# Linear attention: the inverted normalizer copied to each head's channels by eight DMAs

## The chip, the cores and the metric

The kernel runs on one core of a Trainium2 chip. The metric is the time of one execution in microseconds, as the device measures it. The program is one launch that computes two transformer layers one phase after the other: softmax attention, a router with 16 experts, linear attention, and a coupling network. The change touches only the third of these.

## What is computed

Of the reference, this is the part that the change is about (here for one sequence; the kernel does it for 8 sequences of 512 tokens with 256 channels, 16 heads of 16 channels each):

```python
q_prime = elu(q) + 1.0
k_prime = elu(k) + 1.0
kv_cumsum = cumsum(einsum('bhld,bhle->bhlde', k_prime, v), axis=2)
context = einsum('bhld,bhlde->bhle', q_prime, kv_cumsum)
k_cumsum = cumsum(k_prime, axis=2)
norm = einsum('bhld,bhld->bhl', q_prime, k_cumsum)
output = context / (norm[..., None] + EPS)
return output.reshape(b, l, e) @ out_w + out_b
```

`norm` has one value for each head and token; the context has 16 channels for each head. So the inverse of `norm` must stand 16 times, once for each channel of its head, before the context can be multiplied by it.

## The kernel before

`linear_phase` (L1357) works through 8 sequences, b = 0 to 7. Every engine runs the same list of steps, built by `placed_order` from the table `LINEAR_PLACE` (L1281): a step of sequence b stands at place 36 b plus its number in the table, so steps of two or three sequences are woven into each other. Each engine does its own part of a step and waits on semaphores for the parts of others. Within an engine everything runs in the order of the list.

The steps are: `ln` SyncE loads x (512 KB) and a gate row; `st` DVE takes the moments of a later sequence; `xn` ACT normalizes; `hT` PE transposes and ACT copies out (two halves); `qk` PE makes q and k, ACT and DVE map them; `v` PE and DVE; `mask` ACT; `nt` the normalizer; `A` PE makes the scores of 128 tokens and DVE masks them (L1612, four instructions) in four tiles; `kt`, `KV` the running state; `PV` PE makes the context of 128 tokens in psum and DVE multiplies it by the inverted normalizer into `oN` (L1648); `pr` PE projects (L1833), DVE adds the residual (L1656), and SyncE stores (L1442).

The normalizer goes this way. PE sums over each head's channels (L1760): the result has heads and token tiles in its partitions, row 32 i + 8 k + h for token tile i, channel half k and head h of that half, and 128 tokens in the free dimension. DVE adds 1e-6 and inverts it into `rinv` (L1599, L1603, semaphore `inverted`). GpSimd multiplies it by a mask that leaves one block of rows for each token tile (`rdiag`, L1522). In step `nb`, two halves k, PE multiplies a constant 0/1 matrix by `rdiag` (L1767), which puts each head's row on its 16 channels for all 512 tokens, in psum bank 6 (`ps_x`), and ACT copies that to `rb` (L1722, `l_norm_rows` in the trace). The first `PV` of the sequence on DVE waits for that copy.

Psum bank 6 is shared by `hT`, `qk`, `nb` and `kt`: each of them on PE waits until ACT has copied out the one before. Psum bank 7 (`ps_y`) is shared by `v`, `nt` and `pr` in the same way with DVE.

In the order around the change the steps of a sequence b run: `nt`, `kt`, `KV`, `v`, `A` 0, `nb` 0, `pr` 2 of b-1, `hT` 0 of b+1, `A` 1, `pr` 3 of b-1, `nb` 1, `PV` 0, `hT` 1 of b+1, `A` 2, `KV` 1, `pr` 0, `PV` 1, and then `qk` and `v` of b+1. On SyncE's queue stand, from this stretch, the stores of `pr` and the load of b+2, which waits for `pr` 3 of b-1. After `pr` 3 of sequence 0 the queue also issues nine loads of the next phase's weights (L1447), and after `pr` 3 of sequence 2 one load of 1 MB (L1451).

Of the kernel before, what the change touches and what calls it, by code (L numbers as in the profile page):

```python
# [24 lines left out]
P = 128  # L25
# [13 lines left out]
C_SPREAD = C_HEADS + KC * 32  # L39
C_TILES = C_SPREAD + KC * P  # L40
C_END = C_TILES + NT

# [16 lines left out]
def shape_constants():  # L59
# [14 lines left out]
    for k in range(KC):  # L74
        c[i, C_HEADS + k * 32 + 8 * k + i // HD] = 1
        for h in range(8):
            c[i % 32 == 8 * k + h, C_SPREAD + k * P + h * HD:C_SPREAD + k * P + (h + 1) * HD] = 1
    c[i, C_TILES + i // 32] = 1
# [37 lines left out]
def placed_order(table, count, steps, sequences):  # L116

    def place(s):
        at = table[s[0]]
        for n in s[1:]:  # L120
            at = at[n]
        return at

    assert len(steps) == count
    order = [(count * b + place(s), (s[0], b) + s[1:]) for b in range(sequences) for s in steps]
    return [s for _, s in sorted(order)]
# [878 lines left out]
def expert_phase(nc, m):  # L1005
# [284 lines left out]
    "nb": [48, 53],  # L1290
# [8 lines left out]
def linear_steps():  # L1299

    steps = [("ln",), ("st",), ("xn",), ("nt",)]
    steps += [(kind, n) for kind in ("hT", "mask", "nb") for n in range(2)]
    steps += [(kind, n) for kind in ("qk", "v", "A", "PV", "pr") for n in range(4)]
    return steps + [(kind, n) for kind in ("kt", "KV") for n in range(NT - 1)]
# [52 lines left out]
def linear_phase(nc, m):  # L1357
# [4 lines left out]
    x_use, _ = index_of(order, ("hT", "qk", "nb", "kt"))  # L1362
    y_use, _ = index_of(order, ("v", "nt", "pr"))
    QK_PLACE = {2: 0, 0: 1, 3: 2, 1: 3}
    with ExitStack() as ctx:
# [24 lines left out]
        rdiag = sb("l_norm_diag", [P, NT, P])  # L1390
# [15 lines left out]
        spread = m.const[:, C_SPREAD:C_SPREAD + KC * P].rearrange("p (k c) -> p k c", k=KC)  # L1406
        tiles = m.const[:, C_TILES:C_TILES + NT]
# [11 lines left out]
        placed = sem("lin_norm_placed")  # L1419
# [8 lines left out]
        with nc.Block() as block:  # L1428
            @block.sync
            def _(sp):  # L1430
                for s in order:
                    if s[0] == "ln":
# [5 lines left out]
                        sp.dma_start(rowb[:, b % 3, :], m.mod_rows[b:b + 1, ROW_GATE_L1 * C:(ROW_GATE_L1 + 1) * C].to_broadcast([P, C])).then_inc(in_loaded[b % 3], 16)  # L1438
                    if s[0] == "pr":
# [14 lines left out]
            def _(pool):  # L1454
# [18 lines left out]
                def step(s):  # L1473
# [40 lines left out]
                    if s[0] == "nt":  # L1514
                        b = s[1]
                        pool.wait_ge(inverted, b + 1)
                        settle(pool, m.passed)
                        if b:

                            pool.wait_ge(x_fill, x_use[("nb", b - 1, 1)] + 1)  # L1520
                            settle(pool, m.passed)
                        pool.tensor_tensor(rdiag[:], rinv[:].unsqueeze(1).to_broadcast([P, NT, P]),  # L1522
                                           tiles.unsqueeze(2).to_broadcast([P, NT, P]), ALU.mult).then_inc(placed, 1)
# [14 lines left out]
            def _(dve):  # L1538
# [17 lines left out]
                def step(s):  # L1556
# [39 lines left out]
                    if s[0] == "nt":  # L1596
# [4 lines left out]
                        if b:  # L1601
                            dve.wait_ge(placed, b)
# [35 lines left out]
                    if s[0] == "PV":  # L1638
# [3 lines left out]
                        if i == 0:  # L1642

                            dve.wait_ge(x_drain, x_use[("nb", b, 1)] + 1)
# [17 lines left out]
            def _(act):  # L1662
                def step(s):
# [52 lines left out]
                    if s[0] == "nb":  # L1716
                        _, b, k = s
                        act.wait_ge(x_fill, x_use[s] + 1)
                        if b >= 2:

                            act.wait_ge(o_norm, NT * (b - 1))
                        act.activation(rb[:, b % 2, k, :], ps_x, ACT.Copy).then_inc(x_drain, 1)  # L1722
# [5 lines left out]
            def _(pe):  # L1728
                def step(s):
# [33 lines left out]
                    if s[0] == "nb":  # L1763

                        _, b, k = s
                        pe.wait_ge(placed, b + 1)
                        pe.matmul(ps_x, spread[:, k, :], rdiag[:].rearrange("p i t -> p (i t)"), start=True,  # L1767
                                  stop=True).then_inc(x_fill, 1)
# [656 lines left out]
```

## Time and profile before

| | us |
|---|---|
| median of 3 runs (1177.37 to 1180.38) | 1179.05 |
| span of the profiled execution, first to last instruction | 1175.3 |
| what lies around the span (median less span) | 3.75 |
| linear attention, from about 720 to 983 in the span | 263 |
| PE busy over the span | 1067.3 (91%) |
| DVE, ACT, GpSimd busy | 734.6, 596.7, 467.8 |

All times in the trace are from the start of the span. The time of the profiled execution as a whole is not listed apart from its span, so the 3.75 us around it are taken from the median of the runs. An engine's busy time in a stretch says how close it is to being the limit there; the idle time ahead of an instruction in the timeline, and what ended it, says for whom it waited.

### The profile page before, as it was taken

Reading aid. Unit: us, or ns where it says so; the run is one execution under the profiler, and the core shown is the slowest. Engines: PE = TensorE matmul, PEld = TensorE weight load, DVE = VectorE, ACT = ScalarE, POOL = GpSimd, SP = SyncE. Lnnn points to the kernel's source line nnn. Section 1 sums busy time; section 2 is a strip of 40 time slices with the busy share of each in tenths; the row PEclk is TensorE's granted clock in tenths of the full one; section 3 lists DMA queues with packets and bytes.
Section 4 is the critical chain, followed back from the end, with each engine's and each line's share of the span. In section 5 each row is a group of like instructions: output and inputs, shape, how many; then the busy total and the mean of one; then the engine's idle time right before and its main releaser. Section 6 shows DMA issues by size and latency. Waiting matters only on the chain. (4 is left out here: it accounts for less than half of the span.)

```text
span 1175.3 us, 19800 instructions
## 1 busy us (share of the span) xinstructions
PE 1067.3 (91%) x6630; PEld 603.4 (51%) x6630; DVE 734.6 (63%) x1549; ACT 596.7 (51%) x1133; POOL 467.8 (40%) x692
## 2 busy tenths in 40 slices
PE   5699999999999998479999974899999998999997
PEld 3244455454454443336565642566666665455654
DVE  2867878787787783624332322767787874566756
ACT  3167667676767666113332322443444442876752
POOL 2444635444453511068888874323333420000000
PEclk9599999999999999579999996999999998999999
DMA  4531414233250411436766672021210002001001
GB/s 150 99 58 18 87 37 89 65 70 82 52 105 21 73 40 47 155 103 138 162 162 135 138 154 71 6 65 42 76 39 26 35 15 95 1 10 63 28 28 54
DMA packets 73540, 85.05 MB, mean 72 GB/s; under 512 B 12560, under 2 KB 67800, under 8 KB 73312
## 3 DMA queue, kind: packets, MB, share of 16 engines
q1 hardware_dynamic: 61088, 66.99, 21.9%
q0 software_dynamic: 12288, 16.79, 8.4%
q8 instruction: 54, 0.88, 0.3%
q14 instruction: 46, 0.38, 0.1%
q10 hardware_dynamic: 64, 0.02, 0.0%
HBM read 45.31 MB, written 25.21 MB: 60 GB/s over the span
## 5 line engine op out<-in xcount | busy, mean ns | idle before, releaser
L566 DVE TENSOR_REDUCE nmax<-psum 128x1 f32<-128x512 f32 (+3 forms) x352 | 215.6, 637 | 44.6 <-PE psum L790 39.8
L683 ACT ACTIVATE pT<-psum 128x512 f32<-128x512 f32 x320 | 181.2, 596 | 65.5 <-PE psum L811 35.5
L788 PE MATMUL psum<-k6T,q6T 96*128 96x512 bf16 (+3 forms) x512 | 128.7, 312 | 15.2 <-DVE nmax L566 11.3
L808 PE MATMUL psum<-q6T,k6T 99*128 99x512 bf16 x320 | 119.3, 382 | 1.1 <-ACT pT L683 0.9
L1093 POOL DMA_INDIRECT residual<-expert_y,idx_e x64 | 101.3, 1583 | 25.2 <-issue 17.1
L1612 DVE TENSOR_TENSOR l_scores<-psum,const_sb 128x512 f32<-128x512 f32 x128 | 79.5, 684 | 19.1 <-PE psum L1787 19.0
L788 PEld LDWEIGHTS psum<-k6T,q6T 96*128 96x128 bf16 x512 | 46.0, 100 | 88.4 <-DVE nmax L566 55.2
L790 PE MATMUL psum<-negs_bf,ident_bf 128*128 128x128 bf16 (+2 forms) x352 | 89.0, 253 | 0.0
L823 PE MATMUL psum<-pT,v 128*32 128x512 f32 x640 | 85.0, 604 | 0.0
L1080 POOL DMA_INDIRECT expert_tokens<-router_input,idx_e x64 | 63.2, 987 | 50.0 <-POOLq L913 30.8
L1745 PE MATMUL psum<-l_hT,l_w 128*128 128x512 f32 x128 | 66.4, 643 | 1.6 <-ACT l_hT L1680 0.9
L2252 PE MATMUL psum<-c_x0T,c_w 128*128 128x512 f32 x128 | 62.2, 619 | 0.0
L1147 PE MATMUL psum<-expert_h,expert_w 128*128 128x512 f32 x128 | 61.2, 623 | 0.5 <-ACT expert_h L1193 0.5
L1689 ACT ACTIVATE l_plus_one<-psum,l_bone 128x512 f32<-128x512 f32 x32 | 22.0, 688 | 74.3 <-PE psum L1745 71.8
L1147 PE MATMUL psum<-expert_tokensT,expert_w 128*128 128x512 f32 x128 | 59.1, 604 | 0.3 <-DVE expert_tokensT L1236 0.3
L808 PEld LDWEIGHTS psum<-q6T,k6T 99*128 99x128 bf16 x320 | 31.1, 99 | 46.1 <-ACT pT L683 28.2
L1260 DVE TENSOR_TENSOR expert_y<-expert_weighted,gb_rows 128x256 f32<-128x256 f32 x64 | 27.3, 427 | 40.4 <-ACT expert_weighted L1205 36.3
L1205 ACT ACTIVATE expert_weighted<-psum,par_e 128x256 f32<-128x256 f32 x64 | 30.9, 564 | 41.3 <-PE psum L1175 37.5
L811 PE MATMUL psum<-negt_bf,ident_bf 128*128 128x512 bf16 x128 | 48.6, 380 | 0.0
L1252 DVE TENSOR_SCALAR expert_h<-psum,par_e 128x512 f32<-128x512 f32 x16 | 12.0, 751 | 58.1 <-PE psum L1147 58.1
L2039 POOL TENSOR_SCALAR c_vtmp<-c_mv 128x8 f32<-128x8 f32 x3 | 0.7, 241 | 116.8 <-DVE c_mv L2075 116.8
L2266 PE MATMUL psum<-c_a,c_w 128*128 128x512 f32 x96 | 45.2, 602 | 1.6 <-ACT c_a L2217 1.6
(298 smaller groups left out, 2245.4 us busy)
## 6 DMA issues: line engine op xcount, KB each, us to landing
q6T<-q_parts SPq DMA_DIRECT2D x96, 128.0 KB, 4.3
expert_w<-in_ew SPq DMA_DIRECT2D x16, 768.0 KB
x_in<-in_x SPq DMA_DIRECT2D x8, 512.0 KB, 4.2
residual<-x SPq DMA_DIRECT2D x32, 128.0 KB, 1.9
router_input<-h SPq DMA_DIRECT2D x32, 128.0 KB, 1.8
l_x<-residual SPq DMA_DIRECT2D x8, 512.0 KB, 6.6
x_dram<-l_x SPq DMA_DIRECT2D x32, 128.0 KB, 1.7
out<-c_out SPq DMA_DIRECT2D x16, 256.0 KB, 2.1
```

The lines of the kernel that those rows point to most:

```text
L566: dve.tensor_reduce(nmax[:, i, u * nh:(u + 1) * nh], ps_s[:, n % SR, 0:nh * (i + 1) * P].rearrange("p (h k) -> p h k", h=nh), AX_X, ALU.ma ...
L683: act.activation(pT[:, n % PR].rearrange("p h t -> p (h t)"), ps_t[:, n % TR, :], ACT.Exp, scale=HD ** -0.5).then_inc(probs, 1)
L788: pe.matmul(out[:, a, :], q6T[0:6 * HD, b % 2, u * nh + a, i * P:(i + 1) * P], k6T[0:6 * HD, b % 2, 0:w], start=a == 0, stop=False, skip_g ...
L790: pe.matmul(out[:, :, i * P:w], m.ident_bf[:], m.negs_bf[:].unsqueeze(1).to_broadcast([P, nh, P]), start=False, stop=True, skip_group_chec ...
L808: last = pe.matmul(out, k6T[:, b % 2, j * P:(j + 1) * P], q6T[:, b % 2, hg * 4:hg * 4 + 4, i * P:(i + 1) * P], start=True, stop=j < i)
L823: last = pe.matmul(ps_o[32 * hg:32 * hg + 32, :], v32[:, b % 2, j, :], pT[:, (n + hg) % PR].rearrange("p h t -> p (h t)"), start=j == 0, s ...
L1080: pool.indirect_dma_start(out=tok[:, e % TOK, i, :], out_offset=None, in_=tokens, in_offset=bass.IndirectOffsetOnAxis(ap=m.idx_e[:, e, i:i ...
L1093: pool.indirect_dma_start(out=rows, out_offset=bass.IndirectOffsetOnAxis(ap=m.idx_e[:, e, i:i + 1], axis=0), in_=y[:, e % YS, i, :], in_of ...
L1147: ins = pe.matmul(ps[:, o, :], wts[:, e % 2, n, k, o * P:(o + 1) * P], src[:, k, :], start=k == 0, stop=k == KC - 1)
L1612: dve.tensor_tensor(kept[:, t % 2, r, :].rearrange("p (h t) -> p h t", h=4), ps_a[:, r, :].rearrange("p (h t) -> p h t", h=4), keep.unsque ...
L1745: last = pe.matmul(ps_x, w[:, k, n * P:(n + 1) * P], hT[:, k, :], start=k == 0, stop=k == KC - 1)
L2252: last = pe.matmul(ps_1[:, n % 2, :], w1[:, w, k, h * P:(h + 1) * P], o[:, q % 3, a, k, :], start=k == 0, stop=k == KC - 1)
```

## The change

The step `nb` is gone from the table, and with it GpSimd's block diagonals, the PE multiplications, ACT's copies out of psum and the two constants `spread` and `tiles`. Psum bank 6 has two users less. In their place SyncE, at place `nt`, waits for `inverted` and issues eight DMAs, one for each token tile and channel half: each reads 8 partitions of `rinv` (one row of 128 floats for each of 8 heads) 16 times over and writes 128 partitions of `rb`, 512 bytes each. All count on one semaphore, `spread`. The first `PV` of the sequence on DVE waits until all eight have landed, and so does DVE before it overwrites `rinv` one sequence later.

```diff
-    "nb": [48, 53],
@@ constants
-C_SPREAD = C_HEADS + KC * 32
-C_TILES = C_SPREAD + KC * P
-C_END = C_TILES + NT
+C_END = C_HEADS + KC * 32
@@ sync
+                    if s[0] == "nt":
+                        b = s[1]
+                        sp.wait_ge(inverted, b + 1)
+                        if b >= 2:
+
+                            sp.wait_ge(o_norm, NT * (b - 1))
+                        for i in range(NT):
+                            for k in range(KC):
+                                lo = 32 * i + 8 * k
+                                sp.dma_start(rb[:, b % 2, k, i * P:(i + 1) * P],
+                                             rinv[lo:lo + 8, :].unsqueeze(1).to_broadcast([8, HD, P])).then_inc(spread, 16)
@@ gpsimd
-                        pool.tensor_tensor(rdiag[:], rinv[:].unsqueeze(1).to_broadcast([P, NT, P]),
-                                           tiles.unsqueeze(2).to_broadcast([P, NT, P]), ALU.mult).then_inc(placed, 1)
@@ vector, step nt
                         if b:
-                            dve.wait_ge(placed, b)
+                            dve.wait_ge(spread, 16 * NT * KC * b)
                         dve.reciprocal(rinv[:], npe[:]).then_inc(inverted, 1)
@@ vector, step PV
                         if i == 0:
 
-                            dve.wait_ge(x_drain, x_use[("nb", b, 1)] + 1)
+                            dve.wait_ge(spread, 16 * NT * KC * (b + 1))
@@ scalar
-                        act.activation(rb[:, b % 2, k, :], ps_x, ACT.Copy).then_inc(x_drain, 1)
@@ tensor
-                        pe.matmul(ps_x, spread[:, k, :], rdiag[:].rearrange("p i t -> p (i t)"), start=True,
-                                  stop=True).then_inc(x_fill, 1)
```

On PE, from `A` 0 of a sequence in the middle to `pr` 0, this is the order before (L1787 is `A`, L1767 `nb`, L1833 `pr`, L1740 `hT`, L1821 `PV`, L1800 `KV`):

```order
1609 L1787 MATMUL psum<-l_q_masked,l_k 128x256 x8
1610 L1767 MATMUL psum<-l_norm_diag,const_sb 128x512
1611 L1833 MATMUL psum<-l_gwo,l_oN 128x256 x2
1612 L1740 MATMUL psum<-const_sb,l_xn 128x128 x4
1613 L1787 MATMUL psum<-l_q_masked,l_k 128x256 x8
1614 L1833 MATMUL psum<-l_gwo,l_oN 128x256 x2
1615 L1767 MATMUL psum<-l_norm_diag,const_sb 128x512
1616 L1821 MATMUL psum<-l_scores,l_v 32x128 x16
1617 L1740 MATMUL psum<-const_sb,l_xn 128x128 x4
1618 L1787 MATMUL psum<-l_q_masked,l_k 128x256 x8
1619 L1800 MATMUL psum<-l_v,l_k_tokens 128x128 x2
1620 L1833 MATMUL psum<-l_gwo,l_oN 128x256 x2
```

and this is the same stretch of PE in the change, whose lines stand some 8 to 21 lower in the file:

```order
1605 L1766 MATMUL psum<-l_q_masked,l_k 128x256 x8
1606 L1812 MATMUL psum<-l_gwo,l_oN 128x256 x2
1607 L1725 MATMUL psum<-const_sb,l_xn 128x128 x4
1608 L1766 MATMUL psum<-l_q_masked,l_k 128x256 x8
1609 L1812 MATMUL psum<-l_gwo,l_oN 128x256 x2
1610 L1800 MATMUL psum<-l_scores,l_v 32x128 x16
1611 L1725 MATMUL psum<-const_sb,l_xn 128x128 x4
1612 L1766 MATMUL psum<-l_q_masked,l_k 128x256 x8
1613 L1779 MATMUL psum<-l_v,l_k_tokens 128x128 x2
1614 L1812 MATMUL psum<-l_gwo,l_oN 128x256 x2
```

The two multiplications into bank 6 are gone; nothing else on PE has changed its place.

On SyncE's queue, for the sequences 2 and 3, the change has (L1444 are the stores of `pr`, L1428 and L1429 the load of a later sequence, L1439 the new copies):

```order
228 L1428 DMA l_x<-residual 128x4x256 [waits lin_vector_bank_drained]
229 L1429 DMA l_rows<-mod_rows 128x256
230 L1444 DMA x3_dram<-l_x3 128x256 [waits lin_vector_bank_drained] x2
231 L1439 DMA l_norm_rows<-l_norm_inv 128x1x128 [waits lin_out_normalized,lin_norm_inverted]
232 L1439 DMA l_norm_rows<-l_norm_inv 128x1x128 x7
233 L1444 DMA x3_dram<-l_x3 128x256 [waits lin_vector_bank_drained] x2
234 L1428 DMA l_x<-residual 128x4x256 [waits lin_vector_bank_drained]
```

where before there were four stores between the loads:

```order
225 L1437 DMA l_x<-residual 128x4x256 [waits lin_vector_bank_drained]
226 L1438 DMA l_rows<-mod_rows 128x256
227 L1442 DMA x_dram<-l_x 128x256 [waits lin_vector_bank_drained] x4
228 L1437 DMA l_x<-residual 128x4x256 [waits lin_vector_bank_drained]
```

The eight copies stand between the second and the third store.

## Rows read from the trace of the kernel before

**Rows 1.** The linear phase as one window: busy us (and instructions) of each engine.

```profile
core 0: us, PE busy (x) PEld busy (x) DVE busy (x) ACT busy (x) POOL busy (x), PEclk, DMA share, GB/s
739.00:983.00 244.00, 237.66 (x2344) 158.04 (x2344) 181.94 (x387) 103.41 (x174) 79.04 (x100) 0.99 0.12 39
```

**Rows 2.** The inversion: durations min/median/max in ns, first and last start.

```profile
L1603 DVE RECIPROCAL l_norm_inv<-l_norm x8: 953/954/954, 740.2 to 960.2; 128x128 f32<-128x128 f32 x8
```

**Rows 3.** Timeline of PE, sequence 3: start, us, line, operation, [idle before].

```profile
838.19 1.10 PE L1767 MATMUL psum<-l_norm_diag,const_sb 128*128 128x512 f32 x2
839.13 1.03 PE L1833 MATMUL psum<-l_gwo,l_oN 128*128 128x256 f32 x4
...
840.56 1.33 PE L1787 MATMUL psum<-l_q_masked,l_k 32*128 32x256 f32 x16
...
842.79 1.02 PE L1767 MATMUL psum<-l_norm_diag,const_sb 128*128 128x512 f32 x2
843.74 1.08 PE L1821 MATMUL psum<-l_scores,l_v 128*32 128x128 f32 x32
...
846.42 0.71 PE L1800 MATMUL psum<-l_v,l_k_tokens 128*128 128x128 f32 x4
846.97 1.03 PE L1833 MATMUL psum<-l_gwo,l_oN 128*128 128x256 f32 x4
...
849.38 1.13 PE L1745 MATMUL psum<-l_hT,l_w 128*128 128x512 f32 x2
```

**Rows 4.** Timeline of DVE, sequence 3.

```profile
835.78 0.95 DVE L1603 RECIPROCAL l_norm_inv<-l_norm 128x128 f32<-128x128 f32 x1
...
838.23 2.48 DVE L1612 TENSOR_TENSOR l_scores<-psum,const_sb 128x512 f32<-128x512 f32 x4 [0.70 <-PE psum L1787]
...
841.80 2.49 DVE L1612 TENSOR_TENSOR l_scores<-psum,const_sb 128x512 f32<-128x512 f32 x4 [0.75 <-PE psum L1787]
...
844.89 0.42 DVE L1648 TENSOR_TENSOR l_oN<-psum,l_norm_rows 128x256 f32<-128x256 f32 x1 [0.28 <-PE psum L1821]
846.57 2.49 DVE L1612 TENSOR_TENSOR l_scores<-psum,const_sb 128x512 f32<-128x512 f32 x4 [1.26 <-PE psum L1787]
...
849.63 0.42 DVE L1648 TENSOR_TENSOR l_oN<-psum,l_norm_rows 128x256 f32<-128x256 f32 x1
```

**Rows 5.** SyncE's queue in softmax attention: six copies, SBUF to SBUF.

```profile
25.36 3.92 SPq L323 DMA_DIRECT2D q6T<-q_parts  x6
```

**Rows 6.** Landing of single 8 KB copies (L346) and of 128 KB stores (L1442).

```profile
DMA to landing us min/median/max: 1.7/1.7/2.7
...
DMA to landing us min/median/max: 1.7/1.7/4.6
```

**Rows 7.** Windows (last: DMA share, GB/s): within those six copies; loads from DRAM.

```profile
30.00:31.00 1.00, 0.00 (x0) 0.00 (x0) 0.99 (x2) 0.00 (x0) 0.77 (x4) 0.58 1.12 120
...
849.00:850.00 1.00, 1.00 (x20) 0.56 (x11) 1.00 (x4) 0.00 (x0) 0.00 (x0) 1.00 1.04 344
```

**Rows 8.** Inversions of the sequences 1 and 2, and the wait between them.

```profile
770.01 0.95 DVE L1603 RECIPROCAL l_norm_inv<-l_norm 128x128 f32<-128x128 f32 x1
...
789.65 0.17 DVE L1563 COPY l_cols<-modT 128x4 f32<-128x4 f32 x1 [5.37 <-DMA l_rows<-mod_rows]
...
805.06 0.95 DVE L1603 RECIPROCAL l_norm_inv<-l_norm 128x128 f32<-128x128 f32 x1
```

**Rows 9.** Idle stretches of PE, and PE's windows (busy, clock) after two of them.

```profile
793.89 1.27 PE L1751 MATMUL psum<-l_w,l_hT 128*128 128x256 f32 x4 [2.54 <-DVE l_v L1594]
...
1013.59 0.63 PE L2234 MATMUL psum<-const_sb,c_xn 128*128 128x128 f32 x4 [1.74 <-ACT c_xn L2148]
...
1014.00:1017.00 3.00, 2.84 (x15) 1.00 0.02 5
795.80:799.20 3.40, 3.40 (x24) 0.65 0.00 0
```

**Rows 10.** Step `qk` on PE after `PV` 1, sequence 0.

```profile
752.89 1.98 PE L1745 MATMUL psum<-l_hT,l_w 128*128 128x512 f32 x4
```

More of the change, by code:

```diff
@@ L75, in shape_constants @@
         c[i, C_HEADS + k * 32 + 8 * k + i // HD] = 1
-        for h in range(8):
-            c[i % 32 == 8 * k + h, C_SPREAD + k * P + h * HD:C_SPREAD + k * P + (h + 1) * HD] = 1
-    c[i, C_TILES + i // 32] = 1
     return c
@@ L122, in place @@
         return at
-    assert len(steps) == count
+    assert len(steps) <= count
     order = [(count * b + place(s), (s[0], b) + s[1:]) for b in range(sequences) for s in steps]
@@ L1301, in linear_steps @@
     steps = [("ln",), ("st",), ("xn",), ("nt",)]
-    steps += [(kind, n) for kind in ("hT", "mask", "nb") for n in range(2)]
+    steps += [(kind, n) for kind in ("hT", "mask") for n in range(2)]
     steps += [(kind, n) for kind in ("qk", "v", "A", "PV", "pr") for n in range(4)]
@@ L1361, in linear_phase @@
     order = [s for s in order if s not in LINEAR_LEAD]
-    x_use, _ = index_of(order, ("hT", "qk", "nb", "kt"))
+    x_use, _ = index_of(order, ("hT", "qk", "kt"))
     y_use, _ = index_of(order, ("v", "nt", "pr"))
@@ L1389, in linear_phase @@
         rinv = sb("l_norm_inv", [P, P])
-        rdiag = sb("l_norm_diag", [P, NT, P])
         rb = sb("l_norm_rows", [P, 2, KC, T])
@@ L1405, in linear_phase @@
         heads = m.const[:, C_HEADS:C_HEADS + KC * 32].rearrange("p (k h) -> p k h", k=KC)
-        spread = m.const[:, C_SPREAD:C_SPREAD + KC * P].rearrange("p (k c) -> p k c", k=KC)
-        tiles = m.const[:, C_TILES:C_TILES + NT]
         gated = sem("lin_residual_gated")
@@ L1418, in linear_phase @@
         inverted = sem("lin_norm_inverted")
-        placed = sem("lin_norm_placed")
+        spread = sem("lin_norm_spread")
         a_fill = sem("lin_scores_filled")
@@ L1513, in step @@
                         pool.tensor_tensor(qk[:, k, :], qs[:, b % 2, k, :], kc[:, k, :], ALU.mult).then_inc(multiplied, 1)
[L1514 to L1521, printed above, removed]
-                        pool.tensor_tensor(rdiag[:], rinv[:].unsqueeze(1).to_broadcast([P, NT, P]),
-                                           tiles.unsqueeze(2).to_broadcast([P, NT, P]), ALU.mult).then_inc(placed, 1)
                     if s == ("nt", 6):
@@ L1715, in step @@
                         act.activation(ktok[:, i, :], ps_x[:, 0:C], ACT.Copy).then_inc(x_drain, 1)
[L1716 to L1721, printed above, removed]
-                        act.activation(rb[:, b % 2, k, :], ps_x, ACT.Copy).then_inc(x_drain, 1)
                 for s in order:
@@ L1762, in step @@
                         last.then_inc(y_fill, 1)
-                    if s[0] == "nb":
-                        _, b, k = s
-                        pe.wait_ge(placed, b + 1)
-                        pe.matmul(ps_x, spread[:, k, :], rdiag[:].rearrange("p i t -> p (i t)"), start=True,
-                                  stop=True).then_inc(x_fill, 1)
                     if s[0] == "kt":
```

## The prediction

> **What bounds the kernel now.** I read first the linear phase as one window [rows 1]: of 244 us PE is busy 237.7, DVE 181.9, ACT 103.4, GpSimd 79.0, and the granted clock is 0.99, that is nearly all at the upper level. PE sets the pace and DVE is not far behind; ACT and GpSimd have room. Second, the timeline of PE over the stretch that the change touches [rows 3], to see what a `nb` multiplication takes of PE's time: it starts at 838.19 and the next operation at 839.13, so 0.94 us; the other runs from 842.79 to 843.74, 0.95 us. Third, DVE in the same stretch [rows 4], to see what else would hold the sequence up once PE is quicker: DVE idles 0.70, 0.75, 0.28 and 1.26 us, each time for PE. Fourth, how much time lies between the inversion and its first use. The inversion of sequence 3 starts at 835.78 and takes 0.95, so it is done at 836.73 [rows 2, 4]; the first `oN` starts at 844.89, 8.2 us later. I count all times of a sequence from the end of its inversion, and call S the time from there until the last of the eight copies has landed. Everything hangs on S.
>
> **What is removed.** Sixteen multiplications on PE, 0.94 + 0.95 = 1.9 us for each of 8 sequences, 15.1 us in all, on the engine that is busy nearly all the time. Not all of it is gained, since DVE takes over. I lay the steps end to end without `nb`, for sequence 3. `A` 0 still ends on DVE at 838.23 + 2.48 = 840.71; the last quarter of `A` 1 on PE waits for that psum bank, so `A` 1 on DVE can start some 0.4 us later, at about 841.2 and not 841.80 [rows 4]: 0.6 us. `PV` 0 and `hT` 1 on PE then follow without the second `nb` and start 1.2 earlier; `A` 2 on DVE comes 1.1 us earlier than 846.57, and `KV` 1, `pr` 0, `PV` 1 and `qk` (849.38) with it [rows 3, 4]. So a sequence gains about 1.1 us as long as the copies are not waited for. The rest of the 1.9 us goes into waiting for DVE's masks. The copies out of psum on ACT and the product on GpSimd cost nothing now: both engines are under half busy [rows 1], and with them gone nothing is shorter but the chain through PE. The smaller constant table is loaded in the first microseconds of the program, long before linear attention, beside larger loads; I cost it at nothing.
>
> **What is added: S.** SyncE has nothing to do at that place (its queue waits for `pr` 1, which is done before, and the guard on `oN` of two sequences ago is long past), so the first issue follows the inversion at once. Two things can then limit S.
>
> The issues. Six SBUF-to-SBUF copies take 3.92 us of the queue [rows 5], 0.65 each. The eighth issue starts after 7 x 0.65 = 4.6 us, and a single small copy, like a 128 KB store, lands 1.7 us after its issue [rows 6]: S = 6.3. If an issue costs a quarter more, 7.4.
>
> The transfer. The eight copies write 8 x 64 KB = 512 KB. With data from DRAM to all partitions the DMA engines move 344 GB/s at a full share [rows 7]; at that rate 512 KB take 1.5 us and the issues hide them. But the six copies in softmax attention, whose one side is 16 partitions, keep the engines just as busy (share 1.12) and move 120 GB/s [rows 7]: a third. Whatever the cause, it goes with few partitions on one side. That is 7.5 GB/s for each of 16 partitions. Here the narrow side has 8 partitions, the source, so 60 GB/s: 524,288 bytes take 8.7 us, and with 1.7 us for start and receipt S = 10.4. The rows in the new copies are 512 bytes where those had 1 KB, which can only slow them; I allow an eighth more, 9.8 us and S = 11.5, and take 10.7. No row has reads from 8 partitions and writes to 128, so the two ends are 6.3 (nothing to pay for the narrow side) and 11.5; I take a value near the upper one, because the copies of rows 7 are the only SBUF-to-SBUF copies with a queue of others behind them.
>
> The Trainium skill, SBUF — State Buffer, section "Door 1: The DMA port swizzle", says that DMA bandwidth goes by how many of 16 ports the partitions reach, at 27.2 GB/s each, four neighbouring partitions to a port. By that the copies in softmax attention (16 partitions, 4 ports) would run at 109 GB/s, and the trace's 120 is near it; eight partitions are two ports, 54.4 GB/s, an estimate of 9.6 us for the transfer and S = 11.3 by that page. The Trainium skill, DMA: Bandwidth & Descriptors, "Why a DMA increments its semaphore by 16 and not by 1", adds that a copy runs on as many DMA engines as divide the slowest dimension of both sides, which here would be 8 of 16; no row of mine shows that, and alone it would make 3 us, which the issues hide.
>
> **What S does.** DVE runs `oN` at S, then `A` 2 (2.4 us), `state`, `pr` 0 and `oN` 1 at a pitch of 0.33: `oN` 1 starts at S + 3.4. PE waits with `pr` 0 for the first `oN`, S + 0.5, and reaches `qk` 2.4 us later (846.97 to 849.38 [rows 3]), at S + 2.9. Before, `qk` came at 849.38 - 836.73 = 12.65. So a sequence breaks even at S = 9.7, keeps its full 1.1 us below 8.6, and loses S - 9.7 above. What is queued behind the waiting `oN` on DVE is `A` 2, and behind `pr` 0 on PE all of the next sequence's `qk` and `v`.
>
> The eight sequences at S = 10.7:
> - 2, 4, 5, 6: +1.0 each, +4.0.
> - 0: it has no `pr` of a sequence before it, and its `qk` comes at 752.89, 11.7 after the inversion at 741.16 [rows 2, 10]; it breaks even at 8.8: +1.9.
> - 1: DVE waits 5.37 us for the gate row [rows 8], which hangs behind `pr` 3 of sequence 0 and nine weight loads on SyncE's queue. The late `oN` is covered by that wait, and `pr` 3 comes 0.6 earlier: -0.6.
> - 3: a 1 MB load stands before the row that DVE waits for, some slack: +0.3.
> - 7: nothing of a next sequence to fill in; its stretch is as tight as 0's: +1.8.
>
> Sum: +7.4 us. The profiled execution's span 1175.3 becomes 1182.7; with the 3.75 us around it, 1186.5, against the median of 1179.05.
>
> **The rivals.**
> *Hidden copies, faster.* S is 6.3 to 7.4, the issues being the limit. Then 1.1 us for sequences 0, 2, 4, 5 and 6, 0.6 for 1, 0.3 for 3, 0.9 for 7: 7.3 us, 1171.8. For it: the engines move 344 GB/s elsewhere, and landing takes 1.7 us. Against it: the 120 GB/s.
> *Even.* S between 9 and 10.1: what the copies take is what the multiplications gave, within 3.5 us of 1179.
> *Late copies and a falling clock, slower still.* PE is ready for `pr` 0 some 9.2 us after the inversion and starts at S + 0.5, so it idles S - 8.7 us in each sequence. After an idle stretch of 2.54 us [rows 9] the granted clock was 0.65 in the window of 3.4 us that followed, so mostly at the 1.2 GHz level; after one of 1.74 us it stayed at 1.00. The row of 0.65 costs up to 3.4 / 2 = 1.7 us. From sequence 1 to 2 the inversions lie 35.05 us apart [rows 8], from 2 to 3 30.72 [rows 4, 8]: 4.3 more, about the idle 2.54 and 1.7 of slow clock. At S = 11.5 PE would idle 2.8 us in seven sequences: 7 x 1.7 = 11.9 us on top of the 12.8 that the sum gives at that S: 1203.8. It decides from S = 11 or so.
>
> **How the numbers follow.** Late copies without a fall of the clock 0.45 (1183 to 1192), with it 0.15, hidden 0.27, even 0.13. The likeliest is 1186.5. The range leaves out half of the cases with a slow clock and the best end of the hidden ones: 1171 to 1203. Faster by over 0.3% (3.5 us, about what a measurement of this kernel can tell from no change) 0.27, within 0.13, slower 0.60.
>
> **What would show it.** In the profile of the changed kernel: the wait ahead of the first `oN` of each sequence on DVE, put down to a DMA, about 2 us long and none at all if the copies are hidden; the landing of the copies from the inversion on, 10.7 against 6.3; the rate while they run, 55 to 60 GB/s against over 100; PE idle 2 us ahead of `pr` 0; the spacing of the inversions, 31.7 against 29.6 in sequences where it was 30.7; the granted clock in the phase. The sum is wrong if an issue costs much over 0.65 us, if DVE does not take over as I laid it out once `nb` is gone, or if the late copies hold up the load of the sequence after next.

## The result, and the profile after

The changed kernel takes 1182.14 us (median of 20 runs, 1178.54 to 1185.70), the kernel before 1179.03 us in 20 runs made with them (1174.20 to 1180.40). The ratio is 1.0030, with a 95% interval of 1.0020 to 1.0041: slower by 3.1 us. The forecast was slower by 7.4. The sign and the place are as forecast; the size is less than half. By the forecast's own bounds this is its rival "even" (S between 9 and 10.1, within 3.5 us of the kernel before), to which it gave 0.13, and not the late copies that it took for the likeliest (1183 to 1192).

The profiled execution took 1182.26 us with a span of 1180.3, so what lies around the span is 2.0 us, not the 3.75 of the forecast. It is 1.8 to 2.4 us in every profiled execution of this study. The 3.75 came from setting the span of one execution against the median of three: 1175.3 and 2 make 1177.3, the lowest of those three.

The linear phase of the changed kernel as one window, against [rows 1] (busy us and instructions of PE, PEld, DVE, ACT, GpSimd; clock; DMA share; GB/s):

```profile
739.00:988.00 249.00, 235.65 (x2314) 158.19 (x2312) 181.70 (x388) 95.21 (x161) 71.49 (x92) 0.99 0.21 55
```

ACT and GpSimd have lost work, and the DMA share went from 0.12 to 0.21. PE has lost the sixteen multiplications, which the forecast costed at 15.1 us, but its busy time fell by only 2 us. A part of what it waits for is counted as busy: in `A` 1 of sequence 3 the same 16 matmuls take 2.33 us and not 1.33 [rows 3], because the later ones wait for DVE to mask a psum bank, and the profile shows no idle time there. So PE's busy share does not say how much work it has left.

```profile
842.32 2.33 PE L1766 MATMUL psum<-l_q_masked,l_k 32*128 32x256 f32 x16
```

DVE in sequence 3, against [rows 4]:

```profile
838.53 0.95 DVE L1595 RECIPROCAL l_norm_inv<-l_norm 128x128 f32<-128x128 f32 x1
...
840.98 2.48 DVE L1604 TENSOR_TENSOR l_scores<-psum,const_sb 128x512 f32<-128x512 f32 x4 [0.70 <-PE psum L1766]
...
844.33 2.48 DVE L1604 TENSOR_TENSOR l_scores<-psum,const_sb 128x512 f32<-128x512 f32 x4 [0.54 <-PE psum L1766]
...
849.01 0.42 DVE L1640 TENSOR_TENSOR l_oN<-psum,l_norm_rows 128x256 f32<-128x256 f32 x1 [1.86 <-issue]
849.36 2.47 DVE L1604 TENSOR_TENSOR l_scores<-psum,const_sb 128x512 f32<-128x512 f32 x4
...
852.41 0.42 DVE L1640 TENSOR_TENSOR l_oN<-psum,l_norm_rows 128x256 f32<-128x256 f32 x1
```

The inversion is done at 839.48. The first `oN` starts 9.53 us later, after 1.86 us of idle time that the kernel before did not have (0.28 there). `oN` 1 follows at 3.40, as laid out in the forecast. The releaser reads "issue", that is, nothing the profile could name. In sequence 0 it names the DMA, and the whole wait is there:

```profile
752.14 0.42 DVE L1640 TENSOR_TENSOR l_oN<-psum,l_norm_rows 128x256 f32<-128x256 f32 x1 [2.30 <-DMA l_norm_rows<-l_norm_inv]
```

PE in the same stretch of sequence 3, against [rows 3]. It reaches `pr` 0 (L1812) with the first `oN`:

```profile
848.30 0.71 PE L1779 MATMUL psum<-l_v,l_k_tokens 128*128 128x128 f32 x4
849.54 1.10 PE L1812 MATMUL psum<-l_gwo,l_oN 128*128 128x256 f32 x4 [0.53 <-issue]
```

All eight sequences, from the DVE timeline (S here is the time from the end of the inversion to the start of the first `oN`; the spacing is from one end of an inversion to the next, for sequence 7 to the first PE operation of the next phase):

| sequence | first `oN`, before | S, after | spacing before | spacing after | difference |
|---|---|---|---|---|---|
| 0 | 7.32 | 9.51 | 29.80 | 30.60 | +0.80 |
| 1 | 8.16 | 9.89 | 35.05 | 35.35 | +0.30 |
| 2 | 8.16 | 9.81 | 30.72 | 30.90 | +0.18 |
| 3 | 8.16 | 9.53 | 31.40 | 32.72 | +1.32 |
| 4 | 8.75 | 9.85 | 31.30 | 32.01 | +0.71 |
| 5 | 8.45 | 9.47 | 30.89 | 30.73 | -0.16 |
| 6 | 8.30 | 9.64 | 30.87 | 30.73 | -0.14 |
| 7 | 8.16 | 9.57 | 22.24 | 22.77 | +0.53 |

The sum is +3.5 us, close to the timed 3.1. (The spans differ by 5.0; the other 1.5 lies before the first inversion, in phases the change does not touch, and that point moves by 7 us, from 737.6 to 744.7, over the profiled executions of this study.)

What SyncE does in sequence 3, its queue in order (start, time taken by the issues):

```profile
839.51 6.42 SPq L1439 DMA_DIRECT2D l_norm_rows<-l_norm_inv  x8
845.98 1.89 SPq L1444 DMA_DIRECT2D x_dram<-l_x  x2
847.96 0.38 SPq L1453 DMA_DIRECT2D c_x_first<-x_dram  x1
848.38 0.66 SPq L1428 DMA_DIRECT2D l_x<-residual  x1
849.09 0.53 SPq L1429 DMA_DIRECT2D l_rows<-mod_rows  x1
```

The eight issues take 6.42 us, 0.80 each. The loads of sequence 5 and the 1 MB load stand behind them, and DVE pays for it when it wants the gate row: 2.66 us of wait before, 3.96 now:

```profile
856.78 0.17 DVE L1555 COPY l_cols<-modT 128x4 f32<-128x4 f32 x1 [3.96 <-DMA l_rows<-mod_rows]
```

The copies themselves, from the DMA view of sequence 0 (the digits are the share of 16 engines in tenths, 0.2 us each; then packets, and the queue's share of the 8 us):

```profile
DMA  0000023333335434333433334334733435333442
...
DMA packets 1059, 0.54 MB, mean 67 GB/s; under 512 B 59, under 2 KB 1057, under 8 KB 1057
...
q1 hardware_dynamic: 1057, 0.51, 32.9%
```

From the first to the last packet of the eight copies it is 7.3 us here and 7.8 to 8.2 in the other sequences, 512 KB at 64 to 72 GB/s. The first packet starts 1.3 us after the first issue, and `oN` starts some 0.4 us after the last packet (0.8 in sequence 0). The stream has no gap: a copy is still running when the next is issued. A packet takes 0.329 x 16 x 8 us / 1057 = 40 ns in the mean.

### The profile page after: what moved, and what is told of

It is laid out like the page before. It is cut to its first block and busy times, and to the rows that moved or that the text cites. A ratio compares the mean times of both kernels' runs of the same rounds, so it can differ in the third digit from the quotient of the medians.

```text
span 1180.3 us, 19739 instructions
## 1 busy us (share of the span) xinstructions
PE 1064.9 (90%) x6598; PEld 603.3 (51%) x6598; DVE 733.6 (62%) x1549; ACT 586.6 (50%) x1117; POOL 458.9 (39%) x684
## 5 line engine op out<-in xcount | busy, mean ns | idle before, releaser
L783 PE MATMUL psum<-k6T,q6T 96*128 96x512 bf16 (+3 forms) x512 | 128.6, 311 | 15.1 <-DVE nmax L561 11.2
L1766 PE MATMUL psum<-l_q_masked,l_k 32*128 32x256 f32 x512 | 47.9, 405 | 0.0
```

The costliest lines, as they stand in the source:

```text
L783: pe.matmul(out[:, a, :], q6T[0:6 * HD, b % 2, u * nh + a, i * P:(i + 1) * P], k6T[0:6 * HD, b % 2, 0:w], start=a == 0, stop=False, skip_g ...
```

## The experiments

Theory A: the transfer of the copies sets S, S costs the wait of `oN`, and the copies also hold up the loads behind them. Theory B: the issues on one queue set S. Theory C: the time goes elsewhere (the clock, or PE and DVE without `nb`). Within A it is open what makes the transfer slow: the bytes, the eight source partitions, or the DMA engines. The kernel before ran beside all of them, and each ratio is against it on the same chip. It took 1175.2 to 1178.7 us there and not always the 1179.03 from which the expectations start, so differences count and not times.

**1. Copies left out.** SyncE's eight issues are gone, and so is DVE's wait for them before the next inversion. `rb` is filled with ones once by GpSimd, so the division is left out of the computation.

```diff
-                        for i in range(NT): (eight copies)
+                        pass
+                pool.memset(rb[:], 1.0).then_inc(spread, 1)
-                            dve.wait_ge(spread, 16 * NT * KC * (b + 1))
+                            dve.wait_ge(spread, 1)
```

> The change without the eight copies: the tile of the inverted normalizer is filled with ones once by GpSimd, so the division is left out. It shows what the removal alone is worth. By the sum of the prediction the sequences gain 1.1 us but for 1, 3 and 7: 1171.8; if the replayed gain of 1.1 is right the inversions lie 29.6 us apart where they lay 30.7. If PE's 1.9 us were gained in full: 1164.

Measured: 1172.58 us, ratio 0.9956 (0.9938 to 0.9973), by the ratio 5.2 us less than the kernel before. The forecast had 7.3 less for hidden copies. What the change removes is worth somewhat less than it was costed at: the spacings are 29.35, 29.87 and 30.18 for 0, 2 and 5, against 29.80, 30.72 and 30.89, so 0.45, 0.85 and 0.71 us and not 1.1. Theory C, in the form that PE and DVE give nothing back, is out.

**2. Half of the issues on ACT.**

```diff
-                            for k in range(KC):
+                            for k in range(1):
@@ scalar, step nt
+                        act.wait_ge(inverted, b + 1)
+                        for i in range(NT):
+                            for k in range(1, KC):
+                                act.dma_start(rb[:, b % 2, k, i * P:(i + 1) * P], ...).then_inc(spread, 16)
```

> The change, with the copies of channel half 1 issued by ACT and those of half 0 by SyncE, four each; the same bytes from the same partitions. In the change S, from the end of the inversion to the first oN, was 9.5 to 9.9 us, and eight issues took 6.4 to 6.9 us of SyncE's queue. If the issues set S (0.81 us each, one queue): four of them take 3.3 us, S falls by about 3 us to 6.5 or so, oN is no longer waited for, and the time is near 1173. If the transfer sets S (reading from 8 partitions): S stays within 0.5 us of 9.5 and the time is 1181 to 1184; ACT's own work has room for four issues in either case.

Measured: 1211.15 us, ratio 1.028 (1.0256 to 1.0304). ACT in sequence 1:

```profile
775.43 3.83 ACTq L1710 DMA_DIRECT2D l_norm_rows<-l_norm_inv  x4
779.36 0.38 ACT L1718 ACTIVATE l_k_tokens<-psum 128x256 f32<-128x256 f32 x1 [6.55 <-issue]
779.64 2.06 ACT L1663 ACTIVATE l_xn<-l_x,l_nbias,l_rstd 128x256 f32<-128x256 f32 x4
```

ACT waits in its order for the inversion and then spends 3.83 us on four issues (3.8 to 4.9 over the sequences). Its copy of `kt`, its `xn` and `hT` stand behind them, and PE needs these. My expectation had ACT half idle and took that for room; an engine's idle share is not room at one place of its order. On the question of the transfer this run still speaks: with two queues SyncE's four issues take up to 4.89 us, 1.2 each, and the eight copies still last 6.0 to 6.9 us. That is 76 to 87 GB/s against 64 to 72. If the issues were the limit, the eight copies would last about half as long; they last 1 us less, so the issues are not the limit (against B). S itself (12.7 to 14.2 us in the first seven sequences) says nothing here, since `oN` is late by way of ACT and PE.

```profile
775.42 4.89 SPq L1439 DMA_DIRECT2D l_norm_rows<-l_norm_inv  x4
```

**3. Half the bytes.** Each copy writes 64 of the 128 tokens; the rest of `rb` stays one (GpSimd fills it once), so half of the division is left out.

```diff
-  sp.dma_start(rb[:, b % 2, k, i * P:(i + 1) * P], rinv[lo:lo + 8, :]...[8, HD, P]
+  sp.dma_start(rb[:, b % 2, k, i * P:i * P + P // 2], rinv[lo:lo + 8, 0:P // 2]...[8, HD, P // 2]
```

> The change with each of the eight copies cut to the first 64 of its 128 tokens (256 byte rows; the other half of the tile is filled with ones once, so half of the division is left out). Same number of issues and of rows, half the bytes. If issues or rows set S, it stays at 9.5 and an issue at 0.79 us. If the bytes out of 8 partitions set it, the data of the eight copies take about half of 7.8 us unless the issues hold them, an issue falls to 0.6 as with 16 rows, and S comes to 7.5 or less.

Measured: 1173.27 us in a single execution, too little for a ratio. The issues take 0.60 us each where those of the change have a median of 0.79, and the first `oN` starts 7.6 to 8.3 us after the inversion without a wait, but for sequence 0 (8.03, of it 0.82 of wait). That is the time at which PE has the context ready, so where `oN` does not wait, S no longer tells when the copies landed. The packets do: the eight copies last 5.8 to 6.2 us.

```profile
L1441 SPq DMA_DIRECT2D l_norm_rows<-l_norm_inv x64: 604/605/1054, 739.3 to 961.1; - x64
```

```profile
L1439 SPq DMA_DIRECT2D l_norm_rows<-l_norm_inv x64: 604/790/1560, 742.7 to 971.3; - x64
```

(min/median/max in ns, here and in the change.) So 0.60 us is what an issue costs by itself, and the other 0.19 is the transfer backing up into the queue. This is against B, in which an issue costs the same whatever it moves, and for A.

**4. Sixteen source rows.** The constant of the normalizer makes each head's row twice, so a copy reads 16 neighbouring partitions 8 times over.

```diff
-        c[i, C_HEADS + k * 32 + 8 * k + i // HD] = 1
+        for n in range(2):
+            c[i, C_HEADS + k * 32 + 16 * k + 2 * (i // HD) + n] = 1
-   rinv[lo:lo + 8, :].unsqueeze(1).to_broadcast([8, HD, P])
+   rinv[lo:lo + 16, :].unsqueeze(1).to_broadcast([16, HD // 2, P])
```

> The change, with every head's row of the normalizer made twice by the matmul that sums over channels (the 16 of 32 columns of its constant that were empty are filled), so that each of the eight copies reads 16 partitions 8 times over in place of 8 partitions 16 times. Number of issues, bytes and destination are the same. If the issues set S: S stays 9.2 to 9.8, the time 1181 to 1183. If the reading from few partitions sets it: the data of a copy take half the time, S falls to what the issues leave, 7.5 to 8, and the time is 1172 to 1175.

Measured: 1173.48 us, ratio 0.9957 (0.9942 to 0.9972). S is 7.6 to 7.9, and 8.0 to 8.3 in the sequences 4 to 6, where no copy is waited for; the issue has a median of 0.60, and the eight copies last 5.5 to 6.4 us. Its DMA view over 7 us of sequence 0:

```profile
DMA  0000004575666567565657666666404675665700
...
DMA packets 1154, 0.55 MB, mean 78 GB/s; under 512 B 128, under 2 KB 1152, under 8 KB 1152
```

Two things changed here at once. There are more source partitions, and there are 128 packets under 512 B, 16 a copy, where the change had 59, some 8 a copy (64 with those that land after the window's end). The Trainium skill, DMA: Bandwidth & Descriptors, "Why a DMA increments its semaphore by 16 and not by 1", says that each engine that takes part writes once to the semaphore, and that a copy uses as many engines, up to 16, as divide the slowest dimension of both sides: 8 in the change and 16 here. The trace agrees, 8 and 16 short packets a copy. Which of the two sets the rate is left to the next run.

**5. Eight source rows, four partitions apart.**

```diff
-        c[i, C_HEADS + k * 32 + 8 * k + i // HD] = 1
+        c[i, C_HEADS + k * 32 + k + 4 * (i // HD)] = 1
-   lo = 32 * i + 8 * k
+   lo = 32 * i + k
-   rinv[lo:lo + 8, :].unsqueeze(1)
+   rinv[lo:lo + 29:4, :].unsqueeze(1)
```

> The heads' rows are put four partitions apart (rows k, k+4, ... k+28 of a token tile's 32), so that each copy still reads 8 partitions of 128 floats and writes 128, but the 8 source partitions lie over 32 instead of next to each other; nothing else changes. The copies with 16 source rows were quicker (S 7.6 to 7.9 against 9.5 to 9.9), and two things changed there at once: more and wider spread source partitions, and twice as many 4-byte packets, one per DMA engine that a copy uses, 128 against about 64 for the eight copies. If neighbouring source partitions share a way out (the Trainium skill, SBUF - State Buffer, 'Door 1: The DMA port swizzle'), the wide spacing helps: S below 8.5, no wait of oN beyond 0.6 us, issues near 0.60 us, time near the 0.996 of the kernel before of the 16-row copies. If the limit is that a copy runs on 8 of 16 DMA engines, S stays 9.4 to 10, issues at 0.79, and the time at 1.003 times the kernel before. I give the engines 0.65.

Measured: 1170.84 us, ratio 0.9949 (0.9928 to 0.9970). The engines, to which I had given 0.65, are not the limit. Issues and DMA view, sequence 0:

```profile
L1439 SPq DMA_DIRECT2D l_norm_rows<-l_norm_inv x64: 604/605/1604, 739.8 to 962.2; - x64
```

```profile
DMA  0000005502520540450351252102531940000000
...
DMA packets 1090, 0.55 MB, mean 69 GB/s; under 512 B 64, under 2 KB 1088, under 8 KB 1088
...
q1 hardware_dynamic: 1088, 0.52, 22.1%
```

```profile
747.64 0.42 DVE L1640 TENSOR_TENSOR l_oN<-psum,l_norm_rows 128x256 f32<-128x256 f32 x1 [0.63 <-DMA l_norm_rows<-l_norm_inv]
```

There are 64 short packets, so 8 engines a copy as in the change. The bytes and the number of source partitions are as in the change too. But a packet takes 0.221 x 16 x 8 / 1088 = 26 ns instead of 40, and the digits fall to zero between copies: each is done before the next is issued. The eight copies take 5.0 to 6.0 us, which is their issues, and S is 7.8 (wait 0.63) in sequence 0 and at most 8.3 behind, without a wait for the copies. So the rate hung on which partitions are read: neighbouring ones hinder each other. The Trainium skill, SBUF — State Buffer, "Door 1: The DMA port swizzle", offers a mechanism, four neighbouring partitions to one port: by that page eight neighbours are two ports, and eight rows four apart are eight. The trace agrees with the direction. It does not agree with the page's 54.4 GB/s for two ports: the change reached 64 to 72, and run 2 reached 76 to 87 out of the same rows. That the rows' places matter is shown; that ports are the reason is not, since only two spacings, one and four, were run.

The profiled execution of run 4 and that of run 5 were each the slowest of their kernel's (1178.95 and 1174.63 us), and their sequence 1 is longer than in the kernel before (36.80 and 36.47 against 35.05). PE idled 4.02 and 3.52 us there for the gate row, and the granted clock then was at its lower level for some 6.8 us, against 3.4 in the kernel before. That is 1.7 us more lost, and it comes with the gate row and not with slow copies.

**6. A semaphore for each token tile**, so that `oN` of a tile waits for two copies only.

```diff
-        spread = sem("lin_norm_spread")
+        spread = [sem(f"lin_norm_spread{i}") for i in range(NT)]
-                        if i == 0:
-                            dve.wait_ge(spread, 16 * NT * KC * (b + 1))
+                        dve.wait_ge(spread[i], 16 * KC * (b + 1))
```

> The change, with a semaphore for each token tile, so that each oN waits for its own two copies and not for all eight. Nothing is sent sooner. Both theories of S: the first two copies land some 3.5 to 4.5 us after the inversion, before the first oN can run (7.7 us), so the wait is gone; the sum's 1.1 us a sequence comes in, less what the loads lose behind the copies: 1173 to 1175. If the loss of the change is not in the wait of oN but in the loads that stand behind the copies, the time stays at 1180 or more.

Measured: 1179.26 us, ratio 1.0000 (0.9987 to 1.0012). The wait of `oN` is gone in all sequences, and spacings of 29.36 and 29.87 appear in 0 and 2. But sequence 1 has 36.74 and sequence 3 has 33.67, with waits for the gate row of 6.61 and 5.79 us, and PE goes idle there (`v` after such a wait):

```profile
797.22 2.07 PE L1735 MATMUL psum<-l_w,l_hT 128*128 128x256 f32 x4 [3.79 <-DVE l_v L1586]
...
863.01 1.13 PE L1735 MATMUL psum<-l_w,l_hT 128*128 128x256 f32 x4 [2.96 <-DVE l_v L1586]
```

With `oN` no longer late, the other six sequences gain 4.5 us together, and 1 and 3 lose 4.0: what was gained in front was lost again at the row behind the copies on the queue. I had allowed for a loss at the loads, but only for 1 to 3 us; it is the second part of theory A. It is sequence 3 that the slow copies lengthen (33.67, against 31.04 in run 4 and 31.65 in run 5, where they are quick); sequence 1 is as long in runs 4 and 5.

**7. The kernel before with the eight copies added**, into a tile that nobody reads. No `oN` waits for them, only the next inversion and the end of the phase.

```diff
+        ru = sb("l_norm_unused", [P, 2, KC, T])
@@ sync, step nt
+                        sp.wait_ge(inverted, b + 1)
+                        for i in range(NT):
+                            for k in range(KC):
+                                sp.dma_start(ru[:, b % 2, k, i * P:(i + 1) * P], ...).then_inc(copied, 16)
```

> The kernel before, all of it, and beside it the same eight copies into a tile that nobody reads; no oN waits for them (only the next inversion and the end of the phase do). It prices the copies' presence alone: eight issues on SyncE's queue ahead of two stores and a load, and their data on the DMA engines. If the copies cost only through the wait of oN: the time of before, within 0.1%. If they hold up the load of the sequence after next: DVE's wait for the gate row in sequence 3, 2.66 us before and 3.96 in the change, comes to about 4, the inversions 3 to 4 lie 32.5 us apart and not 31.4, and the time is 1 to 3 us above before.

Measured: 1177.23 us against 1175.15 for the kernel before, ratio 1.0019 (1.0009 to 1.0029). All spacings are those of the kernel before but two: after sequence 3 it is 32.99 instead of 31.40, after sequence 1 35.23 instead of 35.05. The wait for the gate row is 4.25 us where it was 2.66:

```profile
851.66 0.17 DVE L1576 COPY l_cols<-modT 128x4 f32<-128x4 f32 x1 [4.25 <-DMA l_rows<-mod_rows]
```

This prices the copies as a load on the queue and the DMA engines alone: 2 us, 1.6 of them in sequence 3. `oN` does not wait here.

**8. Twelve copies instead of eight**, all waited for.

```diff
+                        for i in range(NT):
+                            lo = 32 * i
+                            sp.dma_start(ru[:, b % 2, 0, i * P:(i + 1) * P], ...).then_inc(spread, 16)
-                            dve.wait_ge(spread, 16 * NT * KC * (b + 1))
+                            dve.wait_ge(spread, 16 * NT * (KC + 1) * (b + 1))
```

> The change with four copies more for each sequence into a tile that nobody reads, and oN waiting for all twelve. S rises from 9.6 to about 12.8. By the sum of the prediction (each us of S above 9.7 is a us for a sequence, sequence 1 covered by its wait for the gate row) seven sequences lose about 3.1 us more: 1182 + 22 = 1204 with a clock that stays up. PE then idles about 4 us a sequence; if the clock falls after most of these, 1.7 us each more, 1210 to 1216. If DVE or the loads give slack that the sum left out, below 1200.

Measured: 1227.94 us, ratio 1.0453 (1.0438 to 1.0469). S is 14.0 to 15.1, so each added copy costs 1.1 to 1.3 us. The time is more than forecast in two ways: the copies are longer than my line predicted (S 14 and not 12.8), and the clock fell for longer. `oN` and `pr` 0 in sequence 0, and PE in the window behind:

```profile
752.15 0.42 DVE L1645 TENSOR_TENSOR l_oN<-psum,l_norm_rows 128x256 f32<-128x256 f32 x1 [6.81 <-DMA l_norm_unused<-l_norm_inv]
```

```profile
752.67 0.77 PE L1817 MATMUL psum<-l_gwo,l_oN 128*128 128x256 f32 x1 [5.52 <-issue]
```

```profile
751.60:758.40 6.80, 5.72 (x42) 0.55 0.06 20
```

PE idles 5.52 us up to 752.67, and the granted clock is 0.55 over the 6.8 us from 751.6 on, nearly all at the lower of its two levels. It falls so in every sequence, for as long in all but one, where it is half of that (mean clock over the span 0.935 instead of 0.953). The forecast's third rival is a real mechanism, and it costs more than the 1.7 us that I gave it: 6.8 us at half speed lose 3.4. In the change PE's idle time ahead of `pr` 0 is at most 1.0 us, and in no sequence did the clock fall behind it.

**9 and 10. The next phase's loads moved**, in the kernel before and in the change. The nine weight loads go from behind `pr` 3 of sequence 0 to behind `pr` 0 of sequence 1, and the 1 MB load from `pr` 3 of sequence 2 to `pr` 0 of sequence 3, so that they no longer stand ahead of a gate row.

```diff
-                    if s == ("pr", 0, NT - 1):
+                    if s == ("pr", 1, 0):
-                    if s == ("pr", 2, NT - 1):
+                    if s == ("pr", 3, 0):
```

> The kernel before with only the two moves of the next phase's loads. The gate row of sequence 1 then is not waited for (5.37 us before) and the clock does not fall behind it: 35.05 us between the inversions come to 30.7, those of sequence 3 from 31.4 to 30.7 or so: 1179 - 4.3 - 0.7 = 1174. It tells how much of the run before this one belongs to the copies and how much to the loads.

> The change as it is, with only the two moves of the next phase's loads that took the kernel before from 1175.2 to 1170.4. The gate rows are out of the way here, so what is left is the wait of oN. By the sum with the S that was measured (9.5 to 9.9 and a point of balance at 9.7): 0 to 0.2 us for a sequence, 0.7 for 0 and 7, in all 1.5 us above the same kernel with the old normalizer: 1171 to 1173. If the change's loss was in the wait of oN after all and not in the loads: 3 us above, 1174 or more.

Measured: the kernel before 1170.42 us, ratio 0.9962 (0.9949 to 0.9974); the change 1171.74, ratio 0.9972 (0.9956 to 0.9987). The waits for the gate row are gone in both, and with them more than half of the difference of the two: 1.2 us are left (0.0010 of the time; the intervals overlap, but the phase is 0.9 us longer in the traces too). S in the change is 9.4 to 10.2 here too. So 1.2 us is the net of the two: what the late `oN` costs, less what the removal of `nb` gives. Sequence 1 in the kernel before with its loads moved, where the inversions were 35.05 apart [rows 8]:

```profile
766.48 0.95 DVE L1603 RECIPROCAL l_norm_inv<-l_norm 128x128 f32<-128x128 f32 x1
...
797.20 0.95 DVE L1603 RECIPROCAL l_norm_inv<-l_norm 128x128 f32<-128x128 f32 x1
```

30.72 us now. I had expected 5.0 us less than the kernel before, and it is 4.7 less (1170.42 against 1175.15). My figure of 1174 started from 1179.

**11. Sixteen rows and a semaphore for each tile**, loads where they were.

> 16 rows to a copy and a semaphore for each tile, the loads of the next phase where they were. 16 rows alone gave 0.9957 of before, tile by tile alone 1.000. The wait of oN is gone in both, so together they add nothing to 16 rows alone: 0.995 to 0.997, that is 1170 to 1172 beside a before of 1175.2, with the waits for the gate row in sequences 1 and 3 of 6 to 7 and 3 to 4 us. If the semaphores by tile gain by themselves: below 0.993.

Measured: 1172.54 us, ratio 0.9977 (0.9962 to 0.9992): nothing beyond run 4, and slightly above the 0.995 to 0.997 that I expected. Once the copies are quick, splitting their wait is worth nothing.

**12. Both, with the loads moved.**

> The change with 16 rows to a copy and a semaphore for each tile, as in the two runs before, and with the nine weight loads of the next phase and its 1 MB load moved on SyncE's queue behind the load of the sequence after next (to the place of pr 0 of sequence 1, and of sequence 3). If what held back the tile-by-tile waits was the gate row behind those loads in sequences 1 and 3: the waits of 6.6 and 5.8 us for it go to below 1, the inversions lie 30 us apart everywhere, and against the 1173.5 of 16 rows alone some 7 us go from sequence 1 and 1 to 2 from 3: 1164 to 1167. If only the copies mattered: 1172 to 1174.

Measured: 1164.88 us, ratio 0.9906 (0.9890 to 0.9923), against 1175.15 for the kernel before: quicker than both kernels. The phase as one window, against the first of this part:

```profile
739.00:980.00 241.00, 236.38 (x2318) 159.35 (x2317) 184.25 (x395) 96.68 (x165) 68.57 (x90) 0.99 0.26 66
```

The phase itself ends at 971 here; the rest of the window is the next one. All spacings are 29.4 to 30.5. So to take `nb` out pays, 5.5 us against the kernel before with the same loads moved (1170.42), when the copies are quick and don't stand in anybody's way. By the traces it is 0.44 us in sequence 0, 0.86 in the next six and 0.66 in the last, 6.2 us in all. And against run 10, where the copies are slow, it is some 7 us (1171.74 against 1164.88; 7.1 by the traces). That is what the late `oN` costs. Run 5's spacing of rows has not been tried with the moved loads; it needs no second row for each head.

## Why the prediction was wrong in size and right in sign

- **What is removed: right in kind, a quarter too high.** A part of the 1.9 us goes into waiting for DVE's masks, as laid out (`A` 1 takes 2.33 us and not 1.33). What is left is some 0.86 us a sequence and not 1.1, and 0.44 in sequence 0 (runs 1 and 12). With the copies left out (run 1) 7.3 us were forecast and 5.2 measured.
- **S: the step that failed, a term mis-sized.** The forecast took 10.7; the trace has 9.5 to 9.9. I took 7.5 GB/s for each narrow-side partition from the copies in softmax attention [rows 7] and so 60 GB/s, and then added an eighth for the shorter rows. It was 64 to 72 GB/s, 7.3 to 8.2 us from first to last packet, where the forecast had 9.0. No run shows the added eighth, and even the 8.7 us without it was too long; the 1.7 us for start and receipt came out right. The line that a copy costs in proportion to its number of partitions had no ground: run 5 reads just as few and is as quick as its issues. What counts is that they are neighbours. The mis-sized S accounts for 6.2 us of the forecast's 7.4, as the next but one point adds up.
- **The issues: half right.** An issue costs 0.60 us alone (I had 0.65), and 0.79 in the change, because the transfer backs up into it. The forecast kept the two limits apart; here the slower one lengthens the other, and the eight issues take 6.4 to 6.9 us.
- **The break-even at S = 9.7: right.** Sequences 2, 5 and 6 have S of 9.81, 9.47 and 9.64 and differ by +0.18, -0.16 and -0.14. For the sequences 2, 4, 5, 6, 0 and 7 the forecast's terms add up to 7.7. With the measured S in its own line (S - 9.7, and S - 8.8 in 0 and 7) they become 0.1 + 0.15 - 0.2 - 0.1 + 0.7 + 0.8 = 1.5; measured are 0.18 + 0.71 - 0.16 - 0.14 + 0.80 + 0.53 = 1.9.
- **Sequences 1 and 3: wrong, and the other way.** The forecast had -0.6 and +0.3, measured are +0.30 and +1.32. It passed over what the copies do to the loads behind them on SyncE's queue, though it named it at its end as a thing that would break the sum. Run 7 gives it alone: 1.6 us in sequence 3. Of the 3.1 us, by run 7 some 2 are the loads, and by runs 9 and 10 some 1.2 are the late `oN` less the gain of the removal. The two errors go against each other. With S right and this one left in, the forecast would have been 1.5 - 0.3 = 1.2 us; that the sign came out clearly is in part luck.
- **The clock: as far as it went, right.** PE idled at most 1.0 us ahead of `pr` 0, and the rival's price did not come in. In run 8, with S of 14, it did: the forecast's line (S - 8.7) gives 5.3 us of idle time and the trace has 5.52, but all falls but one cost twice the 1.7 us of the forecast. Sequence 4 of the change has one window at 0.61 that the kernel before had not.

```profile
879.00:882.40 3.40, 3.40 (x42) 0.61 0.52 133
```

That window follows an idle time of only 0.52 us ahead of `pr` 3 of sequence 3, and PE is busy throughout. The kernel before has the same idle time (0.51) and no fall; what let the clock fall stays open. It costs up to 1.7 us and is probably most of sequence 4's +0.71: in run 10 S was even longer there (10.15), the clock stayed at 1.00, and the spacing was 31.24 against 31.30 in the kernel before.
- **A slip in the third rival.** By the forecast's own terms the sum at S = 11.5 is 12.2 (7.4, and 0.8 more for each of the six sequences that grow with S), not 12.8. Nothing hangs on it.
- **The time around the span** was 2.0 and not 3.75 us; it does not move the difference.

## What to carry to other kernels

Before an edit puts copies on a queue, list what stands behind them there, and look for the waits that end on those rows. Here the copies cost some 7 us at their own reader, about what the removal gave, and 2 us more at the loads behind them; those 2 were two thirds of the loss. When a copy fans a few SBUF partitions out to many, try the source rows four apart instead of side by side; here that change of a constant and of the rows that a copy names turned 1.0030 into 0.9949. An engine that is half idle has no room for DMA issues unless its order has a gap at that place.

## What the runs showed of the hardware that was not expected

- 512-byte packets out of 8 neighbouring partitions take 40 ns in the mean, out of 8 partitions four apart 26 ns, with the same 8 DMA engines a copy. Out of 16 neighbours with 16 engines a copy they take 45 ns (0.466 x 16 x 7 us / 1152), but twice as many run at once: the eight copies take 5.5 to 6.4 us against 5.0 to 6.0.
- The length of one idle stretch of PE does not by itself tell whether the clock falls. Ahead of the same matmul, behind the gate row of sequence 1, PE idled 2.54 us in the kernel before and 2.76 in the change, and the clock was at its lower level for 3.4 us. In runs 3 to 6 PE idled 3.5 to 4.0 us, and it was there for 6.8. In run 1 it stayed at 1.00 after 3.38 us:

```profile
792.54 0.70 PE L1734 MATMUL psum<-l_w,l_hT 128*128 128x256 f32 x2 [3.38 <-DVE l_v L1584]
```

```profile
792.50:796.00 3.50, 3.46 (x20) 1.00 0.00 0
```

- An issue takes 0.60 us where the copy before it is done, 0.80 to 0.87 in the mean where copies out of neighbouring rows back up (the change), and 0.95 to 1.2 on each of two queues that issue such copies side by side (run 2).
- Matmuls that wait for a psum bank between themselves can count as busy: 2.33 us against 1.33 for the same sixteen (the change, `A` 1). PE's busy time fell by 2 us when 15 us of its work were taken out.
